# Second attention of a two-layer kernel: VectorE's order of work in a slot, its idle copies, and who makes which keep-mask

## The chip, the cores and the metric

The kernel runs on one core of one Trainium2 chip. The metric is the device time of one execution in microseconds. The engines have queues of their own and run in their order: TensorE (PE in the profile) multiplies matrices, VectorE (DVE), ScalarE (ACT) and GpSimd (POOL) work on elements, and SyncE (SP) starts transfers. They meet only in semaphores, on which an instruction waits and which another one counts up.

## The reference, cut to what matters

The whole model is two layers of attention and a mixture of experts on an input of 4 x 1024 x 128. The change lies in the attention of the second layer, which keeps for each query the best 30% of its keys:

```python
def _L1_attn_ref(x, W_qkv, b_qkv, W_out, b_out):
    ...
    topk = max(1, int(Tx * 0.3))
    ...
    scores = jnp.einsum('bhid,bhjd->bhij', q, k) * scale
    topk_scores, indices = jax.lax.top_k(scores, topk)
    ...
    masked = jnp.full_like(scores, -jnp.inf)
    masked = masked.at[bi, hi, ti, indices].set(topk_scores)
    attn = jax.nn.softmax(masked, axis=-1)
    out = jnp.einsum('bhij,bhjd->bhid', attn, v)
    ...
    return out @ W_out.T + b_out
```

There are 4 sequences of 1024 tokens and 16 heads of 8 columns. A query keeps 307 of 1024 keys.

## The kernel before, in words

Each part of the model is a block in which every engine has its own list of instructions. The second attention is `attention1`. It works on 512 tiles; a tile is one head's 128 queries against all 1024 keys. Every engine runs the same loop over slots, written out at build time: in slot h it does the first step of tile h and later steps of earlier tiles. The constants name the lags: VectorE writes z of tile h-1 (`C2`), finds the tops of tile h-2 (`TOPL`), sorts those of tile h-3 (`SORT`), picks the edge for four tiles up to h-5 (`HIT`) in slots with h % 4 == 0; masks are made for tile h-15 (`PICK`), and TensorE and ScalarE use them for tile h-16 (`TURN`). The order of a slot is written by hand.

A tile goes this way. TensorE makes the scores S (L1134, two buffers). ScalarE counts the scores above a first threshold (L1198); GpSimd makes a better threshold from the count (L1259, L1261). VectorE writes z, the scores minus that threshold, from PSUM to SBUF (L1420). ScalarE counts again, on z (L1205). GpSimd subtracts z from a side value, so that the values nearest to the wanted rank come out on top: these are the near values (L1285, two buffers). VectorE finds the eight largest of each quarter of near (`top`, L1381, four MAX8 instructions) and sorts them: the first eight (`sort_first`, L1395), a match-and-replace that takes them out (`sort_rest`, L1403), the next eight (`sort_last`, L1411). The sort of a tile comes one slot behind its tops. From the sorted list and the count VectorE takes the edge (`hits` L1427, `picked` L1433, `edge` L1439), and GpSimd makes the cut from it (L1266).

The keep-mask of a tile has a large negative value where z is below the cut. VectorE makes it with one tensor_scalar (L1458), ScalarE with one Relu with a steep slope (L1213), with the opposite sign; TensorE adds the mask to the transposed scores by a product with an identity (`k.ident_b`) or with minus an identity (`minus_b`) (L1181, L1182). Before, tiles with an even number have their mask from VectorE, in odd slots, and tiles with an odd number from ScalarE, in even slots. There are four mask buffers. ScalarE then takes the exponential (L1220), and TensorE multiplies with v (L1150); every fourth tile ScalarE copies the sum (L1226), TensorE turns it (L1169) and VectorE normalizes it (`reciprocal` L1484, `ctx` L1491).

Four more pieces stand in these queues. `split_max` on GpSimd (L1242 to L1252, in slots with h % 4 == 0, in front of near) splits the row maxima into three bf16 parts; VectorE transposes them (`flip`, L1468) and SP stores them by four transfers into rows of qs, where TensorE reads them in L1181. Once in eight slots, in those with h % 8 == 6, TensorE sums a check of eight tiles (the flag product, L1162; it waits for VectorE's ctx of the same slot), VectorE reads the sum into a register (`value_load`) and branches on it; the branch was taken once in the profiled execution. `idle` is a small tile that nothing reads; `past_waits` copies one element into it (L1414).

In a slot ScalarE's order is: count of tile h, count of z of tile h-1, mask (if it has one), exponential of tile h-16. TensorE's is: S of tile h, a piece of the products with v, the flag product, the turn of the sums, the masked transposed scores of tile h-16. In the rest of this document "slot 6" is any slot with h % 8 == 6, and so on, and tile 7 any tile with number 7 mod 8.

Of the kernel before, what the change touches and what calls it, by code (L numbers as in the profile page):

```python
# [983 lines left out]
def attention1(nc, k, search, ctx_all):  # L984
# [11 lines left out]
    with ExitStack() as ctx:  # L996
# [70 lines left out]
        tile = lambda hl: base(hl) + hl % PAIR // 4 * P  # L1067
        groups = lambda it, h: it * GU + (h - CHECK - 7) // 8
        closes = lambda it, h: lagged(it, h, CHECK, UN, TOTAL) is not None and (h - CHECK) % 8 == 7

# [50 lines left out]
        def _(pe):  # L1121
# [4 lines left out]
            def slot(it, h):  # L1126
# [43 lines left out]
                if lagged(it, h, TURN, UN, TOTAL) is not None:  # L1170
                    l, hl = nth(it, h, TURN), here(h, TURN)
                    pe.wait_ge(mask_a if hl % 2 else mask_s, it * (UN // 2) + (h - TURN) // 2 + 1)
                    if not (isinstance(l, int) and l == 0):
                        pe.wait_ge(e_done, l)
                    if hl % 4 == 0:
                        pe.wait_ge(top_in, 16 * 4 * (it * QU + (h - TURN) // 4 + 1))
                    if isinstance(l, int) and l == 0:
                        pe.wait_ge(ones_in, 16)
                    for kb in range(IB):
                        block_of = slice(kb * P, (kb + 1) * P)  # L1180
                        pe.matmul(ST[:, block_of], ks[:, base(hl) + kb * P:base(hl) + (kb + 1) * P], qs[:, tile(hl):tile(hl) + P], start=True, stop=False)  # L1181
                        mm = pe.matmul(ST[:, block_of], mask[:, hl % MASKS, block_of],  # L1182
                                       minus_b[:, :] if hl % 2 else k.ident_b[:, :], start=False, stop=True)
                    mm.then_inc(turned, 1)
# [3 lines left out]
        def _(act):  # L1188
            act.wait_ge(pool_const, 4)

            def slot(it, h):
# [8 lines left out]
                if lagged(it, h, C2, UN, TOTAL) is not None:  # L1200
                    l, hl = nth(it, h, C2), here(h, C2) % H
                    act.wait_ge(z_s, l + 1)
                    if not (isinstance(it, int) and l == 0):
                        act.wait_ge(cnt2, l)
                    act.activation(signs[:, 1, :], z[:, hl, :], ACT.Sign, bias=tiny[:, :],  # L1205
                                   accum_out=sgn[1][:, hl:hl + 1]).then_inc(cnt2, 1)
                if lagged(it, h, PICK, UN, TOTAL) is not None and (h - PICK) % 2:
                    l, hl = nth(it, h, PICK), here(h, PICK)
                    act.wait_ge(cut_s, it * QU + (h - PICK) // 4 + 1)
                    act.wait_ge(checked, it * GU + (h - PICK) // 8 + 1)  # L1210
                    if not (isinstance(it, int) and l < MASKS):
                        act.wait_ge(turned, l - (MASKS - 1))
                    act.activation(mask[:, hl % MASKS, :], z[:, hl % H, :], ACT.Relu, bias=cut_steep[:, hl % H:hl % H + 1],  # L1213
                                   scale=-STEEP).then_inc(mask_a, 1)
# [77 lines left out]
        def _(dve):  # L1292
# [74 lines left out]
            def slot(it, h):  # L1367
# [44 lines left out]

                def past_waits(c):
                    dve.tensor_copy(idle[:, 2 * (h % H) + c:2 * (h % H) + c + 1], half[0:1, :])  # L1414

                if has1 is not None:
                    dve.wait_ge(thr1_s, l1 + 1)
                    if h1 % 2 and not (isinstance(it, int) and l1 < H):
                        dve.wait_ge(mask_a, it * (UN // 2) + (h - C2) // 2 - (H // 2 - 1))
                    dve.tensor_scalar(z[:, h1 % H, :], S[h1 % 2][:, :], thr1[:, h1 % H:h1 % H + 1], None, ALU.add, ALU.max,  # L1420
                                      accum_out=zmax[:, h1 % H:h1 % H + 1]).then_inc(z_s, 1)
                if h % 4 == 0:
                    listed()
                    if has4 is not None:
# [3 lines left out]
                                          wide(rank[:, four], WINDOW), ALU.is_equal).then_inc(choice_s, 1)  # L1428
                    sort_first()
                    first_sorted()  # L1430
                    if has4 is not None:
                        dve.wait_ge(choice_s, 2 * q4 + 1)
                        dve.tensor_tensor(picked[:, :, :], hits[:, :, :], best[:, ring4, :], ALU.mult).then_inc(choice_s, 1)  # L1433
                    sort_rest()
                    rest_made()
                    near_made()
                    if has4 is not None:
                        dve.wait_ge(choice_s, 2 * q4 + 2)
                        dve.tensor_reduce(edge[:, four], picked[:, :, :], AX, ALU.add).then_inc(edge_s, 1)  # L1439
                    sort_last()  # L1440
                    top(0)
                    top(1)
# [8 lines left out]
                elif h % 2:  # L1451
                    listed()
                    near_made()
                    if lagged(it, h, PICK, UN, TOTAL) is not None:
                        dve.wait_ge(cut_s, it * QU + (h - PICK) // 4 + 1)
                        if not (isinstance(it, int) and lp < MASKS):
                            dve.wait_ge(turned, lp - (MASKS - 1))
                        dve.tensor_scalar(mask[:, hp % MASKS, :], z[:, hp % H, :], cut[:, hp % H:hp % H + 1], AWAY,  # L1458
                                          ALU.is_lt, ALU.mult).then_inc(mask_s, 1)
                    sort_first()  # L1460
                    top(0)
                    first_sorted()
                    if lagged(it, h, TOPL, UN, TOTAL) is not None and ends(h, TOPL):
                        q, ring = quad(it, h, TOPL), ((h - TOPL) // 4) % 2
                        dve.wait_ge(part_s, PART_STEPS * q + PART_STEPS)
                        if not (isinstance(it, int) and q < 2):
                            dve.wait_ge(top_in, 16 * 4 * (q - 1))
                        dve.transpose(flip[:, ring, :], parts[:, ring, :]).then_inc(flip_s, 1)  # L1468
                    else:
                        past_waits(0)  # L1470
                    sort_rest()
                    top(1)
                    rest_made()
                    past_waits(1)
                    sort_last()
                    top(2)
                    top(3)
                else:
                    q, hn = quad(it, h, NL), here(h, NL + 3) % H
                    norm = lagged(it, h, NL, UN, TOTAL) is not None  # L1480
                    listed()
                    if norm:
                        dve.wait_ge(ot, q + 2)
                        dve.reciprocal(rden[:, hn:hn + 4], heads[:, :, HD]).then_inc(rd, 1)  # L1484
                    sort_first()
                    first_sorted()
                    near_made()
                    if norm:
                        dve.wait_ge(rd, q + 1)
                        dst = ctx_all.rearrange("p t (g c) -> p (t g) c", c=32)[:, bass.ds(q, 1), :].rearrange("p o (j d) -> p (o j) d", d=HD)  # L1490
                        dve.tensor_tensor(dst, heads[:, :, 0:HD], wide(rden[:, hn:hn + 4], HD), ALU.mult).then_inc(normed, 1)  # L1491
                    sort_rest()
                    top(0)
                    rest_made()
                    past_waits(0)
                    sort_last()
                    top(1)
# [6 lines left out]
                    if closes(it, h):  # L1504

                        dve.wait_ge(flag_v, group + 1)
                        past_waits(1)
                        total = dve.value_load(flag_sum[0:1, 0:1].bitcast(I32), min_val=0, max_val=2 ** 31 - 1)
# [742 lines left out]
```

## Time and profile before

| what | value |
|---|---|
| median of three runs | 3609.91 us (3607.0 to 3611.21) |
| profiled execution | 3602.09 us, span 3600.4 us |
| mean granted TensorE clock over the span | 0.779 |
| second attention, first to last z | 1048.3 to 3143.8 us |
| busy over the span: PE, DVE, ACT, POOL | 77%, 76%, 69%, 54% |

The span runs from the first to the last instruction of the profiled execution; its own time is 1.7 us more. A row of the timeline gives the start, the duration, the engine, the line of the kernel, the operation, output<-input with shape and type, and in brackets the idle time of the engine in front of it with what ended it. An instruction's duration can reach beyond the start of the next one on its engine, so a distance from start to start says more of its cost than the duration does. The clock is a share of full speed: 1 is 2.4 GHz, 0.5 is 1.2 GHz.

### The profile page before, as it was taken

Reading aid. Unit: us, or ns where it says so; the run is one execution under the profiler, and the core shown is the slowest. Engines: PE = TensorE matmul, PEld = TensorE weight load, DVE = VectorE, ACT = ScalarE, POOL = GpSimd, SP = SyncE. Lnnn points to the kernel's source line nnn. Section 1 sums busy time; section 2 is a strip of 40 time slices with the busy share of each in tenths; the row PEclk is TensorE's granted clock in tenths of the full one; section 3 lists DMA queues with packets and bytes.
Section 4 is the critical chain, followed back from the end, with each engine's and each line's share of the span. In section 5 each row is a group of like instructions: output and inputs, shape, how many; then the busy total and the mean of one; then the engine's idle time right before and its main releaser. Section 6 shows DMA issues by size and latency. Waiting matters only on the chain. (4 is left out here: it accounts for less than half of the span.)

```text
span 3600.4 us, 75874 instructions
## 1 busy us (share of the span) xinstructions
PE 2754.6 (77%) x23657; PEld 1541.3 (43%) x23705; DVE 2734.2 (76%) x9130; ACT 2480.5 (69%) x4051; POOL 1960.2 (54%) x4543
## 2 busy tenths in 40 slices
PE   4699999677736777777777777776777787757999
PEld 2233333233513454544444545444445454544444
DVE  5777777226448999999999999998999999844444
ACT  2266666433138999999999999997999999832222
POOL 3133333410237777787877777776777777730000
PEclk8699999888656767677777676776776667677999
DMA  5221111010130101101100100110100110010000
GB/s 156 74 53 48 48 53 28 11 33 26 62 54 2 15 3 17 17 2 17 17 7 12 17 14 5 17 15 3 17 11 7 17 15 3 2 31 0 9 6 9
DMA packets 115274, 85.95 MB, mean 24 GB/s; under 512 B 58153, under 2 KB 97339, under 8 KB 114875
## 3 DMA queue, kind: packets, MB, share of 16 engines
q1 hardware_dynamic: 106331, 75.20, 9.7%
q0 software_dynamic: 8192, 4.79, 0.9%
q8 instruction: 185, 3.03, 0.4%
q14 instruction: 214, 1.75, 0.2%
q10 hardware_dynamic: 352, 1.18, 0.1%
HBM read 54.25 MB, written 19.40 MB: 20 GB/s over the span
## 5 line engine op out<-in xcount | busy, mean ns | idle before, releaser
L1285 POOL TENSOR_TENSOR a_near<-a_side,a_z 128x1024 int32<-128x1024 int32 x512 | 968.3, 1891 | 42.7
L1181 PE MATMUL a_ST<-a_qs,a_ks 75*128 75x128 bf16 x4096 | 749.8, 271 | 305.2 <-ACT a_eT L1220 215.3
L1381 DVE MAX8 a_cand<-a_near 128x8 f32<-128x256 f32 x2048 | 778.1, 406 | 2.6 <-POOL a_near L1285 2.5
L1181 PEld LDWEIGHTS a_ST<-a_qs,a_ks 75*128 75x128 bf16 x4096 | 504.8, 125 | 513.7 <-issue 507.0
L1420 DVE TENSOR_SCALAR_CACHE_REDUCE a_z<-a_S,a_thr 128x1024 f32<-128x1024 f32 x512 | 645.6, 1261 | 77.7 <-issue 56.2
L1205 ACT ACTIVATE a_signs<-a_z,a_tiny 128x1024 bf16<-128x1024 f32 x512 | 587.4, 1147 | 152.0 <-DVE a_z L1420 151.2
L1198 ACT ACTIVATE a_signs<-a_S,search 128x1024 bf16<-128x1024 f32 x512 | 569.2, 1112 | 23.1 <-PE a_S L1134 23.0
L1220 ACT ACTIVATE a_eT<-a_ST 128x1024 f32<-128x1024 f32 x512 | 518.7, 1013 | 59.7 <-PE a_ST L1182 59.1
L1134 PE MATMUL a_S<-a_ks,a_qs 72*128 72x512 bf16 x1024 | 438.1, 521 | 99.4 <-DVE a_z L1420 75.6
L775 ACT ACTIVATE a_eT<-a_ST 128x512 f32<-128x512 f32 (+3 forms) x768 | 354.0, 489 | 212.1 <-PE a_ST L745 159.0
L879 DVE TENSOR_REDUCE a_mx<-a_S 128x1 f32<-128x512 f32 (+3 forms) x768 | 380.9, 548 | 92.9 <-PE a_S L732 56.2
L1150 PE MATMUL a_O<-a_eT,a_v 128*9 128x128 f32 x8192 | 404.3, 344 | 1.4 <-ACT wq L1226 1.4
L1182 PE MATMUL a_ST<-ident_b,a_mask 128*128 128x128 bf16 x2048 | 386.1, 277 | 0.0
L1182 PE MATMUL a_ST<-a_minus_b,a_mask 128*128 128x128 bf16 x2048 | 375.4, 271 | 0.0
L1150 PEld LDWEIGHTS a_O<-a_eT,a_v 128*9 128x9 f32 x8192 | 220.4, 107 | 273.0 <-issue 234.6
L1213 ACT ACTIVATE a_mask<-a_z,a_cut_steep 128x1024 bf16<-128x1024 f32 x256 | 290.8, 1136 | 0.0
L1458 DVE TENSOR_SCALAR a_mask<-a_z,a_cut 128x1024 bf16<-128x1024 f32 x256 | 192.5, 752 | 120.0 <-issue 116.4
L1182 PEld LDWEIGHTS a_ST<-ident_b,a_mask 128*128 128x128 bf16 x2048 | 258.9, 126 | 0.1
L1182 PEld LDWEIGHTS a_ST<-a_minus_b,a_mask 128*128 128x128 bf16 x2048 | 253.3, 124 | 0.0
L742 PE MATMUL a_ST<-a_qs,a_ks 128*128 128x512 bf16 (+3 forms) x720 | 232.5, 330 | 18.0 <-ACT a_eT L775 15.0
L2015 ACT ACTIVATE f_gate<-f_G 128x512 f32<-128x512 f32 x112 | 66.8, 597 | 243.5 <-PE f_W L1981 196.0
L1279 POOL TENSOR_TENSOR a_shifted<-a_sgn,a_miss 128x1 f32<-128x1 f32 x512 | 96.3, 188 | 215.1 <-ACT a_signs L1205 214.8
(342 smaller groups left out, 4568.5 us busy)
## 6 DMA issues: line engine op xcount, KB each, us to landing
a_qs<-q_parts SPq DMA_DIRECT2D x174, 64.0 KB
a_ks<-k_parts SPq DMA_DIRECT2D x174, 64.0 KB
a_qs<-a_flip SPq DMA_DIRECT2D x512, 0.8 KB
q_parts<-p_qp SPq DMA_DIRECT2D x48, 128.0 KB, 1.7
k_parts<-p_kp SPq DMA_DIRECT2D x48, 128.0 KB, 1.8
a_qs<-q_parts SPq DMA_DIRECT2D x60, 96.0 KB
a_ks<-k_parts SPq DMA_DIRECT2D x60, 96.0 KB
f_w<-L_ffn_W SPq DMA_DIRECT2D x16, 256.0 KB, 2.9
```

The source lines that it names most:

```text
L775: act.activation(eT[:, gi % 4, p % G, 0:hi - lo], ST[p % 2][:, 0:hi - lo], ACT.Exp, scale=SCALE0).then_inc(e_done, 1)
L879: dve.tensor_reduce(mx[:, lo // CW, col(j) // P + i:col(j) // P + i + 1], S[j][:, 0:hi - lo], AX, ALU.max).then_inc(max_s, 1)
L1134: mm = pe.matmul(S[h % 2][:, lo:lo + CW], qs[0:STACK, tile(h):tile(h) + P], ks[0:STACK, base(h) + lo:base(h) + lo + CW], start=True, stop= ...
L1150: mm = pe.matmul(O[32 * j:32 * j + HD + 1, :], v[:, h0 // PAIR % 2, kb, j * (HD + 1):(j + 1) * (HD + 1)], eT[:, h0 % RING + j, kb * P:(kb ...
L1181: pe.matmul(ST[:, block_of], ks[:, base(hl) + kb * P:base(hl) + (kb + 1) * P], qs[:, tile(hl):tile(hl) + P], start=True, stop=False)
L1182: mm = pe.matmul(ST[:, block_of], mask[:, hl % MASKS, block_of], minus_b[:, :] if hl % 2 else k.ident_b[:, :], start=False, stop=True)
L1198: act.activation(signs[:, 0, :], S[h % 2][:, :], ACT.Sign, bias=first[:, bass.ds(n, 1)], accum_out=sgn[0][:, one]).then_inc(cnt1, 1)
L1205: act.activation(signs[:, 1, :], z[:, hl, :], ACT.Sign, bias=tiny[:, :], accum_out=sgn[1][:, hl:hl + 1]).then_inc(cnt2, 1)
L1220: act.activation(eT[:, hl % RING, :], ST[:, :], ACT.Exp, scale=SCALE1).then_inc(e_done, 1)
L1285: pool.tensor_tensor(near[:, hl % 2, :].bitcast(I32), side[:, one].bitcast(I32).broadcast_to([P, SEQ]), z[:, hl % H, :].bitcast(I32), ALU. ...
L1381: mm = dve.max(found[:, 8 * g:8 * g + 8], near[:, h2 % 2, g * SW:(g + 1) * SW])
L1420: dve.tensor_scalar(z[:, h1 % H, :], S[h1 % 2][:, :], thr1[:, h1 % H:h1 % H + 1], None, ALU.add, ALU.max, accum_out=zmax[:, h1 % H:h1 % H ...
```

## The change

On VectorE, each slot now does the wait for the listed tops and the first sort right behind z. The rest of the front sort (the wait for the first sort and the match-and-replace) follows, and the wait for the near values (`near_made`) comes behind it in all slots; the transpose `flip` of slots with h % 4 == 1 stands in front of it, hits behind it. All copies into `idle` go, but the one in front of the `value_load` of slot 6. ScalarE makes the masks of tiles 1, 3 and 5 of every eight (in slots 0, 2 and 4), VectorE those of the other five (in all odd slots and in slot 6). The waits of TensorE and of VectorE's z on the two mask semaphores count accordingly, and TensorE takes the identity by who made the mask.

```diff
+        by_act = lambda l: l % 2 == 1 and l % 8 != 7
+        acted = lambda l: sum(by_act(x) for x in range(l + 1))
...
-                    pe.wait_ge(mask_a if hl % 2 else mask_s, it * (UN // 2) + (h - TURN) // 2 + 1)
+                    pe.wait_ge(*((mask_a, acted(l)) if by_act(l) else (mask_s, l + 1 - acted(l))))
...
-                                       minus_b[:, :] if hl % 2 else k.ident_b[:, :], start=False, stop=True)
+                                       minus_b[:, :] if by_act(l) else k.ident_b[:, :], start=False, stop=True)
...
-                if lagged(it, h, PICK, UN, TOTAL) is not None and (h - PICK) % 2:
+                if lagged(it, h, PICK, UN, TOTAL) is not None and by_act(nth(it, h, PICK)):
...
-                def past_waits(c):
-                    dve.tensor_copy(idle[:, 2 * (h % H) + c:2 * (h % H) + c + 1], half[0:1, :])
+                def away_made():
+                    if lagged(it, h, PICK, UN, TOTAL) is not None and not by_act(lp):
+                        dve.wait_ge(cut_s, it * QU + (h - PICK) // 4 + 1)
+                        if lp >= MASKS:
+                            dve.wait_ge(turned, lp - (MASKS - 1))
+                        dve.tensor_scalar(mask[:, hp % MASKS, :], z[:, hp % H, :], cut[:, hp % H:hp % H + 1], AWAY,
+                                          ALU.is_lt, ALU.mult).then_inc(mask_s, 1)
...
-                    if h1 % 2 and not (isinstance(it, int) and l1 < H):
-                        dve.wait_ge(mask_a, it * (UN // 2) + (h - C2) // 2 - (H // 2 - 1))
+                    if l1 >= H and by_act(l1 - H):
+                        dve.wait_ge(mask_a, acted(l1 - H))
                     dve.tensor_scalar(z[:, h1 % H, :], S[h1 % 2][:, :], thr1[:, h1 % H:h1 % H + 1], None, ALU.add, ALU.max,
                                       accum_out=zmax[:, h1 % H:h1 % H + 1]).then_inc(z_s, 1)
+                listed()
+                sort_first()
                 if h % 4 == 0:
-                    listed()
+                    first_sorted()
+                    sort_rest()
+                    near_made()
                     if has4 is not None:
...
                         dve.tensor_tensor(hits[:, :, :], odd2[:, :].rearrange("p (o r) -> p o r", o=1).broadcast_to([P, 4, WINDOW]),
                                           wide(rank[:, four], WINDOW), ALU.is_equal).then_inc(choice_s, 1)
-                    sort_first()
-                    first_sorted()
+                    rest_made()
+                    sort_last()
                     if has4 is not None:
...
                         dve.tensor_tensor(picked[:, :, :], hits[:, :, :], best[:, ring4, :], ALU.mult).then_inc(choice_s, 1)
-                    sort_rest()
-                    rest_made()
-                    near_made()
+                    top(0)
                     if has4 is not None:
...
                         dve.tensor_reduce(edge[:, four], picked[:, :, :], AX, ALU.add).then_inc(edge_s, 1)
-                    sort_last()
-                    top(0)
                     top(1)
...
                 elif h % 2:
-                    listed()
-                    near_made()
-                    if lagged(it, h, PICK, UN, TOTAL) is not None:
...
-                    sort_first()
-                    top(0)
-                    first_sorted()
                     if lagged(it, h, TOPL, UN, TOTAL) is not None and ends(h, TOPL):
...
                         dve.transpose(flip[:, ring, :], parts[:, ring, :]).then_inc(flip_s, 1)
-                    else:
-                        past_waits(0)
+                    first_sorted()
                     sort_rest()
-                    top(1)
+                    near_made()
+                    away_made()
                     rest_made()
-                    past_waits(1)
                     sort_last()
-                    top(2)
-                    top(3)
+                    for g in range(SEGS):
+                        top(g)
                 else:
...
-                    listed()
                     if norm:
                         dve.wait_ge(ot, q + 2)
                         dve.reciprocal(rden[:, hn:hn + 4], heads[:, :, HD]).then_inc(rd, 1)
-                    sort_first()
                     first_sorted()
+                    sort_rest()
                     near_made()
                     if norm:
...
                         dve.tensor_tensor(dst, heads[:, :, 0:HD], wide(rden[:, hn:hn + 4], HD), ALU.mult).then_inc(normed, 1)
-                    sort_rest()
+                    away_made()
+                    rest_made()
+                    sort_last()
                     top(0)
-                    rest_made()
-                    past_waits(0)
-                    sort_last()
                     top(1)
                     top(2)
...
-                        past_waits(1)
+                        dve.tensor_copy(idle[:, 2 * (h % H) + 1:2 * (h % H) + 2], half[0:1, :])
```

## Rows read from the trace of the kernel before

**Rows 1.** Stretches: us, busy us (instructions) of each engine, granted clock, DMA share, GB/s

```profile
2000.00:2500.00 500.00, 382.49 (x4214) 246.78 (x4207) 454.54 (x1702) 459.36 (x704) 392.48 (x984) 0.71 0.09 13
...
1648.20:1658.00 9.80, 6.86 (x72) 4.50 (x72) 8.79 (x35) 8.34 (x15) 7.35 (x15) 0.83 0.11 16
2006.20:2016.00 9.80, 8.03 (x69) 4.86 (x61) 8.83 (x33) 7.58 (x13) 6.37 (x13) 0.50 0.05 13
```

**Rows 2.** Waits from 1100 to 3000: us in total, times, longest us

```profile
DVE a_mask L1458 <- issue: 106.9, 173, 1.1
```

**Rows 3.** VectorE's timeline from slot 6 to the next slot 6, lower clock

```profile
2006.21 1.25 DVE L1420 TENSOR_SCALAR_CACHE_REDUCE a_z<-a_S,a_thr 128x1024 f32<-128x1024 f32 x1
...
2007.69 0.19 DVE L1491 TENSOR_TENSOR ctx<-a_OT,a_rden 128x32 f32<-128x32 f32 x1
...
2010.73 1.28 DVE L1420 TENSOR_SCALAR_CACHE_REDUCE a_z<-a_S,a_thr 128x1024 f32<-128x1024 f32 x1 [0.92 <-issue]
...
2015.58 0.80 DVE L1427 TENSOR_TENSOR a_hits<-a_odd,a_rank 128x64 f32<-128x64 f32 x1
...
2020.85 0.75 DVE L1458 TENSOR_SCALAR a_mask<-a_z,a_cut 128x1024 bf16<-128x1024 f32 x1 [0.86 <-issue]
2021.51 0.19 DVE L1395 MAX8 a_best<-a_cand 128x8 f32<-128x32 f32 x1
...
2021.94 0.19 DVE L1468 STREAM_TRANSPOSE a_flip<-a_parts 128x32 bf16<-128x32 bf16 x1
...
2022.19 0.42 DVE L1381 MAX8 a_cand<-a_near 128x8 f32<-128x256 f32 x1
...
2022.58 0.17 DVE L1411 MAX8 a_best<-a_rest 128x8 f32<-128x32 f32 x1
2022.68 0.72 DVE L1381 MAX8 a_cand<-a_near 128x8 f32<-128x256 f32 x2
2023.33 1.25 DVE L1420 TENSOR_SCALAR_CACHE_REDUCE a_z<-a_S,a_thr 128x1024 f32<-128x1024 f32 x1
...
2036.73 0.75 DVE L1458 TENSOR_SCALAR a_mask<-a_z,a_cut 128x1024 bf16<-128x1024 f32 x1 [0.58 <-issue]
...
2039.21 1.25 DVE L1420 TENSOR_SCALAR_CACHE_REDUCE a_z<-a_S,a_thr 128x1024 f32<-128x1024 f32 x1
```

**Rows 4.** GpSimd's timeline in the same period: near and the thr step

```profile
2005.46 1.89 POOL L1285 TENSOR_TENSOR a_near<-a_side,a_z 128x1024 int32<-128x1024 int32 x1
...
2014.40 1.89 POOL L1285 TENSOR_TENSOR a_near<-a_side,a_z 128x1024 int32<-128x1024 int32 x1
...
2018.86 1.89 POOL L1285 TENSOR_TENSOR a_near<-a_side,a_z 128x1024 int32<-128x1024 int32 x1
...
2021.12 0.53 POOL L1261 TENSOR_TENSOR a_thr<-a_scaled,search 128x1 f32<-128x1 f32 x1
```

**Rows 5.** TensorE's timeline in the same period: the flag product

```profile
2008.03 0.75 PE L1162 MATMUL a_OT<-a_signals,ones 128*1 128x176 f32 x2 [1.46 <-DVE ctx L1491]
```

**Rows 6.** ScalarE's timeline in the same period: exp of slot 6, count of slot 2

```profile
2010.64 1.02 ACT L1220 ACTIVATE a_eT<-a_ST 128x1024 f32<-128x1024 f32 x1 [0.85 <-PE a_ST L1182]
...
2024.63 1.15 ACT L1205 ACTIVATE a_signs<-a_z,a_tiny 128x1024 bf16<-128x1024 f32 x1 [0.75 <-DVE a_z L1420]
```

**Rows 7.** VectorE's z in a period at the higher clock

```profile
1648.18 1.25 DVE L1420 TENSOR_SCALAR_CACHE_REDUCE a_z<-a_S,a_thr 128x1024 f32<-128x1024 f32 x1
...
1652.71 1.28 DVE L1420 TENSOR_SCALAR_CACHE_REDUCE a_z<-a_S,a_thr 128x1024 f32<-128x1024 f32 x1 [0.93 <-issue]
...
1680.33 1.25 DVE L1420 TENSOR_SCALAR_CACHE_REDUCE a_z<-a_S,a_thr 128x1024 f32<-128x1024 f32 x1
```

**Rows 8.** ScalarE's timeline in that period: count of tile 6

```profile
1654.04 1.15 ACT L1205 ACTIVATE a_signs<-a_z,a_tiny 128x1024 bf16<-128x1024 f32 x1 [0.28 <-DVE a_z L1420]
```

**Rows 9.** Groups by line on VectorE, 1100 to 3000: xcount, busy us, mean ns, idle

```profile
L1414 DVE COPY a_idle<-a_half 1x1 f32<-1x1 f32 x519 | 63.7, 123 | 0.0
```

**Rows 10.** Groups by line on ScalarE, 1100 to 3000

```profile
L1213 ACT ACTIVATE a_mask<-a_z,a_cut_steep 128x1024 bf16<-128x1024 f32 x231 | 262.3, 1136 | 0.0
```

More of the change, by code:

```diff
@@ L1451, in slot @@
                 elif h % 2:
-                    listed()
-                    near_made()
-                    if lagged(it, h, PICK, UN, TOTAL) is not None:
[L1455 to L1459, printed above, removed]
-                    sort_first()
-                    top(0)
-                    first_sorted()
                     if lagged(it, h, TOPL, UN, TOTAL) is not None and ends(h, TOPL):
@@ L1465, in slot @@
                         dve.wait_ge(part_s, PART_STEPS * q + PART_STEPS)
-                        if not (isinstance(it, int) and q < 2):
+                        if not (isinstance(q, int) and q < 2):
                             dve.wait_ge(top_in, 16 * 4 * (q - 1))
                         dve.transpose(flip[:, ring, :], parts[:, ring, :]).then_inc(flip_s, 1)
-                    else:
-                        past_waits(0)
+                    first_sorted()
                     sort_rest()
-                    top(1)
+                    near_made()
+                    away_made()
                     rest_made()
-                    past_waits(1)
                     sort_last()
-                    top(2)
-                    top(3)
+                    for g in range(SEGS):
+                        top(g)
                 else:
```

## The prediction

> **What bounds the kernel now.** I began with the table of stretches, to see whether one engine fills the second attention. None does: in 500 us VectorE is busy for 454.54, ScalarE for 459.36, GpSimd for 392.48 and TensorE for 382.49, at a granted clock of 0.71 [rows 1]. So work taken from an engine is worth something only where it lies on the chain that paces the loop. The view of waits says what VectorE stands still for: 106.9 us in front of its masks, 173 times in the 1900 us from 1100 to 3000, put down to "issue", that is, to nothing that the view shows [rows 2].
>
> The timelines of one period of eight slots, from z of slot 6 (h mod 8 = 6) to z of the next, name it. They start at 2006.21 and 2039.21, so a period takes 33.00 us [rows 3]. In slot 1 VectorE stands still for 0.86 us and starts its mask at 2020.85; GpSimd makes the near values of tile 7 from 2018.86 for 1.89 us, to 2020.75 [rows 3, 4]. The mask starts 0.10 behind them: the wait called "issue" is the wait for near. Slot 5 has one of 0.58 [rows 3], and 173 waits in some 58 periods are three a period: slots 1, 3 and 5 wait, slot 7 does not.
>
> Followed backwards, the chain of a period is this. VectorE's mask and tops of slot 5 end in z of slot 6; later in that slot comes ctx (2007.69); TensorE's flag product, which stands in front of the transposed scores in its queue, waits 1.46 for ctx and starts at 2008.03 [rows 3, 5]. ScalarE's exp then waits 0.85 for TensorE and starts at 2010.64 [rows 6]. Two counts, the next exp, split_max and near of tile 7 follow, to 2020.75; then mask and tops of slot 1, and z of slot 2 (2023.33), for which ScalarE has waited 0.75 when it counts that tile at 2024.63 [rows 3, 6]. From there ScalarE and GpSimd run on to near of tile 3, and VectorE's mask of slot 5 starts at 2036.73 [rows 3]. Every other queue has slack somewhere in the period; this chain has none.
>
> That holds at the clock's lower level (0.50 in 2006.2 to 2016.0). In the period that starts at 1648.18 the clock is 0.83 [rows 1], and ScalarE waits not for TensorE but for z of slot 7: that z starts at 1652.71, 4.53 behind slot 6's, and the count of tile 6 at 1654.04, after waiting 0.28 [rows 7, 8]. The next period starts at 1680.33: it took 32.15 [rows 7]. So what VectorE does in slot 6 is on the chain as a whole at the higher clock, and at the lower only up to ctx. A mean clock of 0.71 between the levels 0.5 and 1 means 58% of the time at the lower; the mean period is 0.58 x 33.00 + 0.42 x 32.15 = 32.64.
>
> **The change, part by part.** All prices are distances from start to start.
>
> *Sort in front, idle copies out, slots 1 and 5.* Today 2.48 us lie between the start of the mask and the next z (2020.85 to 2023.33; 2036.73 to 2039.21 [rows 3]). Afterwards mask (0.66, 2020.85 to 2021.51), last sort (0.10, 2022.58 to 2022.68) and four tops (two take 0.65, 2022.68 to 2023.33, so 1.30) are left: 2.06. What moves ahead, the first sort (0.10 like the last), transpose and match (0.25, 2021.94 to 2022.19 [rows 3]), takes 0.35, less than the wait that hides it. The gain on the chain is 0.42 in each of the two slots, 0.84 a period. Slot 3 gains as much, but slot 4 then waits for near of tile 2, which ScalarE's queue makes no earlier: counted at nothing; without that wait it would be another 0.42. The moved transpose releases SP's four stores of the row maxima about 0.4 earlier; TensorE needs them fourteen slots later, so nothing waits for them.
>
> *Idle copies.* The 519 copies last 123 ns each [rows 9], but cost less: a top and a copy take 0.39 (2022.19 to 2022.58 [rows 3]) and a top alone half of 0.65, so a copy takes 0.06; nearly nine a period are 0.5. Those of slots 1 and 5 are in the 0.42; the others stand in slots with slack: nothing. Without one, an instruction that needs the sort just issued can start as late as that sort's end, 0.19 behind its start [rows 3], instead of 0.10. The near wait hides that in slots 1, 3 and 5; uncovered it costs 0.09 a slot.
>
> *Slot 6.* near of tile 4 ends 1.14 behind z today (2005.46 + 1.89 = 2007.35 [rows 4]), and ctx starts at 1.48. As VectorE's slot 5 becomes 0.42 shorter and near comes no earlier against it, near will end at about 1.52 and ctx start at 1.61, 0.13 later. From ctx to z of slot 7 today takes 3.04 (2007.69 to 2010.73 [rows 3]); the match leaves (about half of 0.25), a copy leaves (0.06), a mask comes in (0.66): 3.51, so z of slot 7 starts 5.12 behind slot 6's, where today's two periods have 4.52 and 4.53: 0.59 later.
>
> *The mask taken from ScalarE.* One of four a period, 1136 ns [rows 10]. It lies in slot 6, in front of the exp that waits 0.85 for TensorE at the lower clock [rows 6], or of the count that waits for z of slot 7 at the higher [rows 8]. ScalarE only waits longer, so I take nothing; if neither wait were there it would be up to 1.14.
>
> *New waits.* In slots 0 and 4 the near wait moves in front of hits. Today hits takes 0.80 from 2015.58, to 2016.38, 0.09 behind the end of near (2014.40 + 1.89 = 2016.29 [rows 3, 4]): it is held by GpSimd already, so this is a hold that becomes a wait. Behind it stand picked, edge and the tops, whose reader, GpSimd's cut, comes a slot later.
>
> *Mask against GpSimd.* The thr step beside slot 1's mask took 0.53 from 2021.12 [rows 4], while that mask ran to 2021.60. The Trainium skill ("SBUF — State Buffer", section "SBUF: two separate sides") says that VectorE's instructions in a two-port mode or with two SBUF inputs share an exclusive lock with GpSimd's, and the loser blocks for the whole instruction; the traced hits and thr agree. By that rule the 64 added masks each hold GpSimd. What such a hold can cost here lies between nothing and the 0.53 of that step a period. I take nothing: it falls in slot 6, in front of near of tile 5, which slot 7 needs, where no mask waits today although z comes 0.59 earlier than it will.
>
> *Sum.* Lower clock: +0.13 - 0.84 = -0.71. Higher clock: +0.59 - 0.84 = -0.25. Mean 0.58 x 0.71 + 0.42 x 0.25 = 0.52 a period. Of 64 periods the first two have no masks: 62 x 0.52 = 32 us. The profiled execution took 3602.1 (span 3600.4), so it would take 3570; the median of the runs shown is 7.8 above it, 3609.9, so I forecast **3578**. If every period came to the lower level it would be 32.29 against 32.64, -22 us (3588); all at the higher, 31.90, -46 us (3564). That is the likeliest case's own range.
>
> **Rivals.**
> - *Held transpose (no change).* In the new order the transpose runs while near is being made. If it were held as hits is, transpose and match (0.25) would come behind near again: 0.17 gained a slot instead of 0.42. Lower clock -0.21, higher +0.25, mean -0.02, -1 us: 3609. For it: hits. Against it: nothing in these rows.
> - *Held sort (slower).* If the whole front sort were held until near ends, 2.06 + 0.25 + 0.10 = 2.41 would stay behind it, 0.07 gained a slot: lower clock -0.01, higher +0.45, mean +0.18, +11 us: 3621. At the higher clock it decides once less than 0.30 of the 0.42 is saved. Against it: hits has two SBUF inputs, the sort's instructions one.
> - *VectorE alone sets the pace.* Were ScalarE's relief to bring near forward everywhere, the near waits (106.9 in 58 periods, 1.84) and copies (0.5) would go and a mask (0.66) come: -1.68 a period, -104 us: 3506. Against it: the chain runs through split_max and near, which lose nothing.
> - *GpSimd held by the added mask, on the chain (no change).* +0.53 x 62 = 33 us on the forecast: 3611.
>
> **Chances.** Forecast 0.55, held transpose 0.13, held sort 0.16, VectorE alone 0.10, GpSimd held 0.06. Under 0.2% (7 us) a measurement of this kernel can't tell from no change. Faster 0.55 + 0.10 = 0.65, same 0.13 + 0.06 = 0.19, slower 0.16. The range, 3550 to 3622, leaves out VectorE alone and the far ends of the rest.
>
> **What the profile would show.** Right: slots 1 and 5 take 2.06 from mask to z; the waits in front of the masks of slots 1, 3 and 5 shrink by about 0.4 but stay, and one appears in slot 4; z of slot 7 comes about 5.1 behind slot 6's; ScalarE waits about 1 us longer in slot 6, though it makes fewer masks; a period takes 32.3 or 31.9. Wrong: a transpose or match longer than 0.2 us while near runs; near waits gone; near of tile 5 late for slot 7; a granted clock well away from 0.71.

## The result, and the profile after

The changed kernel takes 3582.59 us (median of 4 runs, 3578.21 to 3583.92) against 3608.45 for the kernel before (4 runs beside it, 3606.57 to 3611.21): a ratio of 0.9926, with a 95% interval of 0.9908 to 0.9943. It is faster by 26 us; the forecast was 32. The profiled execution took 3578.21 (span 3576.5).

Nearly all of it lies where the prediction put it: from z of slot 6 in the second period to z of slot 6 in the last, 62 periods, the second attention took 2041.41 us before and takes 2016.75 now, 24.66 less; the two spans differ by 23.9. Without the first period and the one with the taken branch, a period takes 32.20 in the mean instead of 32.60.

The table of stretches of the changed kernel (stretch, length, then busy time and count of instructions of PE, PEld, DVE, ACT and POOL, the granted clock, the DMA share and GB/s), in the columns of [rows 1]:

```profile
1500.00:2000.00 500.00, 374.93 (x4278) 241.61 (x4278) 459.73 (x1617) 450.44 (x698) 410.64 (x995) 0.73 0.08 11
...
1995.40:2005.20 9.80, 6.75 (x56) 4.36 (x57) 8.87 (x29) 6.52 (x12) 7.28 (x13) 0.65 0.02 6
2028.00:2037.80 9.80, 6.38 (x70) 4.28 (x70) 8.67 (x29) 7.26 (x12) 7.14 (x13) 0.83 0.11 18
```

VectorE is a little busier (459.73 in 500 us against the 454.54 of [rows 1], with less idle filler and one mask more a period), ScalarE less (450.44 against 459.36). The clock is about where it was: 0.73 here, and before 0.71 in [rows 1] and 0.75 from 1500 to 2000. The two lower rows are the first 9.8 us of two neighbouring periods, one that begins at a lower clock and one at a higher.

The view of waits of the changed kernel, 1100 to 3000 (who waits, for whom, us, times, the longest), answers to [rows 2]:

```profile
DVE a_mask L1420 <- POOL a_near L1287: 49.5, 117, 1.0
...
DVE a_hits L1438 <- POOL a_near L1287: 24.1, 58, 0.4
DVE ctx L1485 <- POOL a_near L1287: 20.5, 114, 0.3
```

The wait that was called "issue" now carries its name, near. It went from 106.9 us and 173 times to 49.5 and 117, two a period instead of three; a new one of 0.4 a period stands in front of hits, in slot 4.

VectorE's timeline of the period that answers to [rows 3], and of the next one:

```profile
1995.44 1.26 DVE L1427 TENSOR_SCALAR_CACHE_REDUCE a_z<-a_S,a_thr 128x1024 f32<-128x1024 f32 x1
...
1997.38 0.19 DVE L1485 TENSOR_TENSOR ctx<-a_OT,a_rden 128x32 f32<-128x32 f32 x1 [0.27 <-POOL a_near L1287]
1997.49 0.75 DVE L1420 TENSOR_SCALAR a_mask<-a_z,a_cut 128x1024 bf16<-128x1024 f32 x1
...
2009.38 0.19 DVE L1464 STREAM_TRANSPOSE a_flip<-a_parts 128x32 bf16<-128x32 bf16 x1
2009.50 0.09 DVE L1405 MATCH_VALUE_LOAD a_rest<-a_best,a_cand 128x8 f32 x1
2009.58 0.17 DVE L1405 MATCH_REPLACE8 a_rest<-a_best,a_cand 128x32 f32<-128x32 f32 x1
2010.47 0.75 DVE L1420 TENSOR_SCALAR a_mask<-a_z,a_cut 128x1024 bf16<-128x1024 f32 x1 [0.71 <-POOL a_near L1287]
...
2012.54 1.27 DVE L1427 TENSOR_SCALAR_CACHE_REDUCE a_z<-a_S,a_thr 128x1024 f32<-128x1024 f32 x1
...
2017.55 0.75 DVE L1420 TENSOR_SCALAR a_mask<-a_z,a_cut 128x1024 bf16<-128x1024 f32 x1
...
2021.71 0.23 DVE L1438 TENSOR_TENSOR a_hits<-a_odd,a_rank 128x64 f32<-128x64 f32 x1 [0.42 <-POOL a_near L1287]
...
2025.91 0.75 DVE L1420 TENSOR_SCALAR a_mask<-a_z,a_cut 128x1024 bf16<-128x1024 f32 x1 [0.46 <-POOL a_near L1287]
...
2027.98 1.27 DVE L1427 TENSOR_SCALAR_CACHE_REDUCE a_z<-a_S,a_thr 128x1024 f32<-128x1024 f32 x1
...
2029.83 0.19 DVE L1485 TENSOR_TENSOR ctx<-a_OT,a_rden 128x32 f32<-128x32 f32 x1 [0.18 <-POOL a_near L1287]
...
2033.31 1.28 DVE L1427 TENSOR_SCALAR_CACHE_REDUCE a_z<-a_S,a_thr 128x1024 f32<-128x1024 f32 x1 [0.92 <-issue]
...
2060.03 1.26 DVE L1427 TENSOR_SCALAR_CACHE_REDUCE a_z<-a_S,a_thr 128x1024 f32<-128x1024 f32 x1
```

GpSimd's near of tile 7 in slot 1, and its thr step beside the added mask of slot 6:

```profile
2008.54 1.89 POOL L1287 TENSOR_TENSOR a_near<-a_side,a_z 128x1024 int32<-128x1024 int32 x1
...
2030.17 0.56 POOL L1263 TENSOR_TENSOR a_thr<-a_scaled,search 128x1 f32<-128x1 f32 x1
```

The first period takes 32.54 (1995.44 to 2027.98), the second 32.05. In slots 1 and 5 mask to z takes 2.07 (2010.47 to 2012.54, 2025.91 to 2027.98), against 2.48. The transpose and the match run beside near of tile 7, which GpSimd makes from 2008.54 to 2010.43, at 0.19 and 0.17: nothing holds them. Slot 3's mask (2017.55) has no wait any more. In slot 6, ctx comes 1.94 behind z in the first period and 1.85 in the second, against 1.48. The 1.85 is the rule: of the 60 periods of the trace that have a ctx there, 59 have it at 1.84 or 1.85, and the period shown first is the one exception. Lower-clock periods of the usual kind take 32.45. In the second period z of slot 7 comes 5.33 behind slot 6's (2027.98 to 2033.31), against 4.53.

ScalarE's exp in slot 6 and its count of tile 6 in the two periods, which answer to [rows 6, 8]:

```profile
2000.32 1.02 ACT L1222 ACTIVATE a_eT<-a_ST 128x1024 f32<-128x1024 f32 x1 [2.33 <-PE a_ST L1184]
...
2034.64 1.15 ACT L1207 ACTIVATE a_signs<-a_z,a_tiny 128x1024 bf16<-128x1024 f32 x1 [0.47 <-DVE a_z L1427]
```

The mask that ScalarE lost became a wait for TensorE of 2.33 instead of 0.85 in the first kind of period. In the second, the count still starts 1.33 behind z of slot 7, as before: it goes with VectorE.

### The profile page after: what moved, and what is told of

The parts are those of the page before. It is cut to its first block and busy times, and to the rows that moved or that the text cites. A ratio compares the mean times of both kernels' runs of the same rounds, so it can differ in the third digit from the quotient of the medians.

```text
span 3576.5 us, 74689 instructions
## 1 busy us (share of the span) xinstructions
PE 2730.8 (76%) x23705; PEld 1518.9 (42%) x23705; DVE 2730.8 (76%) x8652; ACT 2416.1 (68%) x3987; POOL 2005.5 (56%) x4543
## 5 line engine op out<-in xcount | busy, mean ns | idle before, releaser
L1183 PE MATMUL a_ST<-a_qs,a_ks 75*128 75x128 bf16 x4096 | 723.3, 265 | 319.1 <-ACT a_eT L1222 185.7
L1383 DVE MAX8 a_cand<-a_near 128x8 f32<-128x256 f32 x2048 | 740.4, 411 | 2.6 <-POOL a_near L1287 2.6
L1184 PE MATMUL a_ST<-ident_b,a_mask 128*128 128x128 bf16 x2560 | 475.0, 274 | 0.0
L1184 PEld LDWEIGHTS a_ST<-ident_b,a_mask 128*128 128x128 bf16 x2560 | 320.2, 125 | 0.0
L1420 DVE TENSOR_SCALAR a_mask<-a_z,a_cut 128x1024 bf16<-128x1024 f32 x320 | 239.8, 750 | 57.8 <-POOL a_near L1287 53.7
L742 PE MATMUL a_ST<-a_qs,a_ks 128*128 128x512 bf16 (+3 forms) x768 | 247.2, 334 | 15.7 <-ACT a_eT L775 12.9
L1184 PE MATMUL a_ST<-a_minus_b,a_mask 128*128 128x128 bf16 x1536 | 258.8, 257 | 0.0
L1261 POOL TENSOR_TENSOR a_scaled<-a_sgn,search 128x1 f32<-128x1 f32 x512 | 171.6, 335 | 144.9 <-ACT a_signs L1200 143.4
L1215 ACT ACTIVATE a_mask<-a_z,a_cut_steep 128x1024 bf16<-128x1024 f32 x192 | 219.5, 1143 | 0.0
L1184 PEld LDWEIGHTS a_ST<-a_minus_b,a_mask 128*128 128x128 bf16 x1536 | 178.8, 116 | 0.1
```

The costliest lines, as they stand in the source:

```text
L1383: mm = dve.max(found[:, 8 * g:8 * g + 8], near[:, h2 % 2, g * SW:(g + 1) * SW])
```

## The experiments

Each kernel's ratio is to the kernel before on the same chip (3609.79, 3606.99 and 3609.33 us for the three groups of runs: the first four, the next four, the last).

**The order without the new share.** The changed kernel, with masks alternating as before.

```diff
-        by_act = lambda l: l % 2 == 1 and l % 8 != 7
+        by_act = lambda l: l % 2 == 1
```

> The changed kernel with the masks shared as before: ScalarE makes those of tiles 1, 3, 5 and 7 again, VectorE none in slot 6. Chain theory: ScalarE's relief in slot 6 was worth nothing and VectorE's mask there costs at the higher clock, where slot 6 lies on the chain as a whole. z of slot 7 comes 0.66 us earlier (about 4.7 behind slot 6's instead of 5.35). A period stays 32.45 at the lower clock and falls from 32.05 to about 31.4 at the higher: -0.3 on the mean over 62 periods, about 3564 us against 3583 of the changed kernel. Balance theory (the relief of ScalarE is what made the kernel faster, the order little): slower than the changed kernel, 3600 or more.

3563.91 us, ratio 0.9871 (0.9856 to 0.9886), as expected. VectorE's z in a higher-clock period of it (the clock is 0.83 from 1865.9 to 1868.9):

```profile
1864.40 1.27 DVE L1427 TENSOR_SCALAR_CACHE_REDUCE a_z<-a_S,a_thr 128x1024 f32<-128x1024 f32 x1
...
1869.09 1.29 DVE L1427 TENSOR_SCALAR_CACHE_REDUCE a_z<-a_S,a_thr 128x1024 f32<-128x1024 f32 x1 [0.95 <-issue]
...
1895.80 1.26 DVE L1427 TENSOR_SCALAR_CACHE_REDUCE a_z<-a_S,a_thr 128x1024 f32<-128x1024 f32 x1
```

z of slot 7 is back at 4.69 behind slot 6's, and the period takes 31.40; at the lower clock it takes 32.45, as with the new share.

**The share without the order.** The kernel before, with `by_act`, `acted` and the waits of the diff, and slot 6's mask behind ctx.

> The kernel before, order and idle copies as they were, with only the masks shared anew: ScalarE three of eight, VectorE five, the added one in slot 6 behind ctx. Chain theory: lower clock +0.1 a period, higher +0.66 (z of slot 7 later), mean +0.33 x 62 = +20 us, about 3629 us, slower than before by 0.5%. Balance theory: faster than before, by 10 us or more.

3627.66 us, ratio 1.0048 (1.0034 to 1.0062): slower, as expected. Together the two runs say that the order is worth some 46 us and that the share costs 18 to 20 of them.

**ctx in front of the near wait in slots 2 and 6.**

```diff
-                    near_made()
                     if norm:
...
+                    near_made()
                     away_made()
```

> The changed kernel with the wait for the near values moved behind ctx in the slots that normalize (2 and 6); nothing else differs. Chain theory: ctx of slot 6 starts 1.6 us behind z instead of 1.94, the flag product and the exponential behind it come 0.35 earlier, so a period at the lower clock falls from 32.45 to 32.1; at the higher clock only the 0.1 of ctx itself is saved: mean -0.24 x 62 = -15 us, about 3568 us. Rival (the flag product is not on the chain, the low-clock period is set elsewhere): within 4 us of the changed kernel's 3583.

3567.62 us, ratio 0.9886 (0.987 to 0.9901), as expected. VectorE's z and ctx of a lower-clock period, then ScalarE's exp in it:

```profile
1798.60 1.27 DVE L1427 TENSOR_SCALAR_CACHE_REDUCE a_z<-a_S,a_thr 128x1024 f32<-128x1024 f32 x1
...
1800.19 0.18 DVE L1484 TENSOR_TENSOR ctx<-a_OT,a_rden 128x32 f32<-128x32 f32 x1
...
1830.80 1.27 DVE L1427 TENSOR_SCALAR_CACHE_REDUCE a_z<-a_S,a_thr 128x1024 f32<-128x1024 f32 x1
```

```profile
1803.11 1.02 ACT L1222 ACTIVATE a_eT<-a_ST 128x1024 f32<-128x1024 f32 x1 [1.96 <-PE a_ST L1184]
```

ctx starts 1.59 behind z instead of 1.85, and exp still 2.92 behind ctx (2.94 in the changed kernel, 2.95 before); the period falls from 32.45 to 32.20. At the lower clock the place of ctx sets the period, as the prediction's chain has it.

**VectorE's added mask in slot 2 instead of slot 6** (tile 3's instead of tile 7's).

```diff
-        by_act = lambda l: l % 2 == 1 and l % 8 != 7
+        by_act = lambda l: l % 2 == 1 and l % 8 != 3
```

> The changed kernel with another mask moved: VectorE makes that of tile 3 (in slot 2) instead of tile 7 (in slot 6), ScalarE those of tiles 1, 5 and 7. The share is still three and five. Chain theory: slot 6 loses 0.66 (higher clock -0.63 a period, lower nothing); in slot 2 ScalarE's mask stood on the chain between the count of tile 1 and that of tile 2, so up to 1.04 goes there, but z of slot 3 comes 0.66 later and takes most of it: -0.1 at either clock. Mean -0.4 x 62 = -25 us, about 3558 us. Balance theory: no difference to the changed kernel, 3583, since the work of each engine is the same.

3578.25 us, ratio 0.9914 (0.9899 to 0.9929): a miss, 20 us above the expected. Each kind of period is as short as expected, 32.34 and 31.0 to 31.3, but 46 of 61 were of the longer kind and 12 of the shorter. Its table of stretches shows the clock beside it, 0.68 and 0.70 where the changed kernel has 0.73:

```profile
1100.00:1500.00 400.00, 315.79 (x3367) 197.95 (x3367) 367.08 (x1292) 363.07 (x558) 325.86 (x796) 0.68 0.08 10
1500.00:2000.00 500.00, 392.10 (x4279) 245.11 (x4279) 460.06 (x1623) 454.69 (x700) 408.87 (x995) 0.70 0.08 11
```

**ctx first, with masks alternating** (the third edit and the first).

> The two edits that helped, together: the changed kernel's order and no idle copies, the near wait behind ctx in slots 2 and 6, and the masks shared as before (ScalarE four of eight). Chain theory: the two gains lie at different clock levels and add: lower clock 32.45 - 0.35 = 32.1, higher 31.4 or a little under. With half of the periods at either level 31.75 against 32.60 before, 62 x -0.85 = -53 us, about 3556 us. Rival (behind ctx another link is just as late, so that the gains don't add): 3564, like the order alone.

3539.75 us, ratio 0.9815 (0.9802 to 0.9828), 16 below the expected. The longer periods take 32.17, near the expected 32.1; the shorter ones take 31.1 to 31.3, up to 0.3 less than the 31.4 that was expected as the upper end. Of 61 periods 27 are of the shorter kind and 15 of the longer; the others lie between.

**ctx first, with the added mask in slot 2** (the third edit and the fourth).

> The changed kernel with the near wait behind ctx and VectorE's extra mask that of tile 3 (slot 2) instead of tile 7. With tile 3 alone the periods were 31.26 at the higher clock and 32.34 at the lower, but five of six came to the lower level, and that was all its gain. Chain theory: 32.34 - 0.36 = 31.98 at the lower level, 31.2 at the higher; if the shares of the levels stay, 31.85 a period, 62 x -0.75 = -46 us, about 3563 us; if half of the periods come to the higher level, 3547 us. Rival (the place of the mask sets the time, ctx nothing): 3578.

3528.79 us (3524.0 to 3533.2), ratio 0.9784 (0.977 to 0.9797): the fastest version here, 2.2% under the kernel before, and 18 us below the lower of the two times expected. Periods take 31.96 (27 of 61) or 30.87 to 31.1 (29), the latter up to 0.3 less than the expected 31.2. Its clock over a long stretch is no higher than that of the fourth experiment:

```profile
1100.00:2480.00 1380.00, 1100.04 (x11854) 686.96 (x11855) 1285.00 (x4526) 1265.08 (x1944) 1163.28 (x2767) 0.68 0.08 12
```

So the mean clock alone does not tell how many periods are short. The clock in slot 6 does, while TensorE works between ctx and exp. These are the 3 us from 1.5 to 4.5 us behind z of slot 6, in a period of 30.87 and in one of 31.96 of this kernel (columns as above):

```profile
1629.80:1632.80 3.00, 2.48 (x36) 1.50 (x36) 2.27 (x11) 3.00 (x5) 2.60 (x7) 1.00 0.32 49
1692.00:1695.00 3.00, 2.57 (x19) 1.95 (x20) 2.28 (x12) 2.10 (x3) 2.60 (x7) 0.50 0.00 0
```

In that stretch the clock is 1.00 in all 29 of the short periods and 0.50 in all 27 of the long ones; in the fourth run it is 1.00 in the 12 short ones and 0.50 to 0.59 in the 46 long ones.

**The new order in slots 1 and 5 alone.** The kernel before, with first sort, transpose and match in front of the near wait there, and without the copy there; the copies of the other slots and the alternating masks stay.

```diff
+                elif h % 4 == 1:
+                    listed()
+                    sort_first()
...
+                    first_sorted()
+                    sort_rest()
+                    near_made()
...
+                    rest_made()
+                    sort_last()
+                    for g in range(SEGS):
+                        top(g)
                 elif h % 2:
```

> The kernel before with the new order in slots 1 and 5 alone (first sort, transpose, match, near wait, mask, last sort, four tops; the copy there goes); slots 0, 2, 3, 4, 6 and 7 keep their order and their idle copies, and the masks are shared as before. Chain theory: only these two slots are on the chain behind a near wait, so this gives all that the whole new order gives without the new share: 0.8 a period less ctx's later start, about 3564 us. Rival (the gain comes from all slots, a part from each): 3587, half of the way.

3568.58 us, ratio 0.9898 (0.9883 to 0.9914). Expected was all that the whole new order gives. By ratio it is 1.0% of 1.3%, and the two intervals just overlap: most of it, and all of it is not excluded.

**No idle copies, all else as before** (the one ahead of the register load stays).

```diff
-                    else:
-                        past_waits(0)
...
-                    past_waits(1)
...
-                    past_waits(0)
```

> The kernel before with the idle copies taken out but for the one in front of the register load; order and shares as they were. Chain theory: one copy of 0.06 in each of slots 1 and 5 lies on the chain, at the higher clock also the one in slot 6: -0.12 to -0.18 a period, -8 to -11 us, unless the sort's next step then starts later by as much; about 3601 us, between 3598 and 3610. Rival (copies hide the waits): slower than before.

3599.68 us (11 runs), ratio 0.9983 (0.9974 to 0.9992): 6 to 7 us, as two copies of 0.06 on the chain in 62 periods make (7.4).

**One idle copy put back behind near in slots 1 and 5.** The changed kernel, and in front of the mask:

```diff
                     near_made()
+                    if h % 4 == 1:
+                        dve.tensor_copy(idle[:, 2 * (h % H):2 * (h % H) + 1], half[0:1, :])
                     away_made()
```

> The changed kernel with one idle copy put between the near wait and the mask in slots 1 and 5. In the changed kernel the mask starts 0.04 us behind near, so GpSimd's next step (scaled) meets it and takes 0.73, and near of tile 4 ends 3.93 behind near of tile 3 instead of 3.72: that made ctx of slot 6 late. If that hold is the cause, the copy (0.06) lets scaled through first: scaled 0.2, thr 0.5, near of tile 4 at 3.72 to 3.75, ctx of slot 6 at 1.75 to 1.8 behind z instead of 1.94, though VectorE does more. The time changes little: two copies cost 0.12 a period, the earlier ctx gives 0.15 to 0.2 back at the lower clock alone: 3583 to 3588 us. If the hold has nothing to do with it: near of tile 4 keeps its 3.93, and the time rises by 0.12 x 62 = 7 us.

3575.06 us, ratio 0.9904 (0.9888 to 0.9921): 8 us under the expected, and not slower than the changed kernel (0.9908 to 0.9943), though an instruction was added to the chain twice a period. In the mean a period takes 32.15 (32.20 in the changed kernel), which is 3 us of the difference; the rest is not told from noise, as the intervals overlap. GpSimd's timeline around slot 5 says why; first the kernel before, then the changed one, then this one, with VectorE's mask and the ctx behind it:

```profile
2034.74 1.89 POOL L1285 TENSOR_TENSOR a_near<-a_side,a_z 128x1024 int32<-128x1024 int32 x1
...
2036.74 0.19 POOL L1259 TENSOR_TENSOR a_scaled<-a_sgn,search 128x1 f32<-128x1 f32 x1
2037.00 0.53 POOL L1261 TENSOR_TENSOR a_thr<-a_scaled,search 128x1 f32<-128x1 f32 x1
...
2038.46 1.89 POOL L1285 TENSOR_TENSOR a_near<-a_side,a_z 128x1024 int32<-128x1024 int32 x1
```

```profile
2023.98 1.89 POOL L1287 TENSOR_TENSOR a_near<-a_side,a_z 128x1024 int32<-128x1024 int32 x1
2025.83 0.19 POOL L1290 TENSOR_TENSOR a_rank<-a_sgn,a_shifted 128x1 f32<-128x1 f32 x1
2025.97 0.73 POOL L1261 TENSOR_TENSOR a_scaled<-a_sgn,search 128x1 f32<-128x1 f32 x1
2026.79 0.19 POOL L1263 TENSOR_TENSOR a_thr<-a_scaled,search 128x1 f32<-128x1 f32 x1
...
2027.91 1.89 POOL L1287 TENSOR_TENSOR a_near<-a_side,a_z 128x1024 int32<-128x1024 int32 x1
```

```profile
2022.83 1.89 POOL L1287 TENSOR_TENSOR a_near<-a_side,a_z 128x1024 int32<-128x1024 int32 x1
...
2024.82 0.19 POOL L1261 TENSOR_TENSOR a_scaled<-a_sgn,search 128x1 f32<-128x1 f32 x1
2025.09 0.55 POOL L1263 TENSOR_TENSOR a_thr<-a_scaled,search 128x1 f32<-128x1 f32 x1
...
2026.58 1.89 POOL L1287 TENSOR_TENSOR a_near<-a_side,a_z 128x1024 int32<-128x1024 int32 x1
```

```profile
2024.84 0.76 DVE L1420 TENSOR_SCALAR a_mask<-a_z,a_cut 128x1024 bf16<-128x1024 f32 x1
...
2026.91 1.27 DVE L1427 TENSOR_SCALAR_CACHE_REDUCE a_z<-a_S,a_thr 128x1024 f32<-128x1024 f32 x1
...
2028.51 0.19 DVE L1487 TENSOR_TENSOR ctx<-a_OT,a_rden 128x32 f32<-128x32 f32 x1
```

In the changed kernel the mask starts at 2025.91, 0.06 ahead of the scaled step, which then takes 0.73, and from near of tile 3 to near of tile 4 it is 3.93. With the copy the mask starts at 2024.84, 0.02 behind the scaled step; that step takes 0.19, the one after it 0.55, and near to near is 3.75 (3.72 before: 2034.74 to 2038.46). ctx starts 1.60 behind z, near the 1.61 of the prediction. Of the 0.25 by which that is earlier, 0.18 is near's; the rest is z, which comes later because the mask now starts 0.12 behind near instead of 0.04.

## Why the prediction was right, and which terms were off

**The chain of near waits: right.** Of the order's gain the two slots 1 and 5 give most on their own (the seventh run), and each shortens from mask to z by 0.41, for which 0.42 was forecast. The copies are worth 0.06 each on the chain (the eighth run), and slot 4, where hits now waits 0.42 and then takes 0.23, costs nothing that any run shows.

**ScalarE's relief and slot 6's added mask: right.** The first two runs part them: the share alone is slower by 18 us and, taken out of the change, gives 20 back (0.0055 by the two ratios). ScalarE's free time became a wait for TensorE. From ctx to z of slot 7 takes 3.48 (2029.83 to 2033.31), for which 3.51 was forecast.

**ctx of slot 6: the term that was mis-sized.** Forecast +0.13 behind z, measured +0.37 in nearly all periods (1.85 against 1.48) and +0.46 in the one shown first. A slip in the sum is a small part of it: near at 1.14 and 0.42 later is 1.56, not 1.52, so +0.17 would have followed from its own rows. The step that failed is "I take nothing" for a hold of GpSimd by a mask. The prediction looked for the hold under the added mask, in slot 6, and bounded it by the 0.53 of the thr step. There it came, 0.56 for the thr step at 2030.17, and cost nothing, as forecast: in no period of the trace does slot 7's mask wait for near. The hold that cost came under a mask that was there before, slot 5's. In the new order VectorE starts that mask 0.04 behind near instead of 0.10. The seventh run has the 0.04 too and the eighth has 0.09, so it comes with the order of slots 1 and 5 and not with the missing copies; why is not shown. The mask then starts 0.06 ahead of GpSimd's scaled step, where it had started 0.01 ahead (2036.73 and 2036.74), and that step is held for 0.73 instead of 0.19: it ends at 2026.70, just behind the mask (2026.66). No semaphore stands between the two instructions, so here two engines meet otherwise than in a semaphore. The thr step behind it, held for 0.53 before (2037.00), is free again at 0.19. The one costs 0.54 and the other gives back 0.34, so near of tile 4 comes 0.21 later (3.93 against 3.72), and ctx behind it; z of slot 7, forecast at 5.12 behind slot 6's, comes at 5.33 for the same reason. The ninth run moves the mask's start back, and scaled step and near come back with it. The Trainium skill ("SBUF — State Buffer", section "SBUF: two separate sides") has a lock that one side takes while the other blocks for the whole instruction; the 0.73 beside a mask of 0.75 agrees.

**How the sum comes out.** In the period shown, against that of [rows 3]: ctx +0.46; exp to the end of near of tile 7 as before (10.11); from there to z of slot 2, 2.11 instead of 2.58; to slot 5's mask 13.37 instead of 13.40; mask to z 2.07 instead of 2.48; with 0.01 less from ctx to exp that is -0.46, and the period fell from 33.00 to 32.54; with ctx at its usual 1.85 it is -0.55, to 32.45. At the higher clock: +0.80 to z of slot 7, -0.47 from near of tile 7 to z of slot 2, and -0.03 and -0.41 as above, so -0.11, and the period fell from 32.15 to 32.05. The forecast had -0.71 and -0.25. In the mean, 0.40 instead of 0.52 a period: 25 us instead of 32. Two things in this are luck. The masks' earlier start behind near, which was not forecast, gives back 0.07 a period (0.47 and 0.44 where twice 0.42 was forecast) of what the late ctx takes. And the share of 58% at the lower clock, read from a mean clock, gave a mean period of 32.64 where the trace has 32.60, though the periods before are not of two lengths only: of 61, 24 take 33.0, 25 take 31.9 to 32.3, and the others mostly lie between.

**Slot 3's wait: wrong, at no cost.** It was to shrink but stay, and it has gone (2017.55 has none). The period did not shorten for it, as the chain does not run there.

**The rivals.** Held transpose and held sort fell at the 0.19 and 0.17 beside near. VectorE alone as the bound fell too: 1.6 us of near waits a period remain (49.5 + 24.1 + 20.5 in some 59 periods). The held GpSimd was partly true, by another mask than the added one and for 0.21 a period where it is on the chain.

**What stays open.** The share of the two kinds of period. The expectations were right to about 0.1 us for the longer kind, and up to 0.3 too long for the shorter one in the fifth and sixth runs. The fourth run missed because most of its periods were of the longer kind; the fifth and the sixth came out faster in part because the shorter kind was shorter than expected, the fifth also because it had more of it. A period is short where the clock in slot 6 is at the higher level (1.00 against 0.50 in the rows of the sixth run), and the mean clock does not give the share (0.68 in a kernel with half of the periods short, 0.68 to 0.70 in one with a fifth); why the sixth run finds the higher level there more often than the fourth was not settled. That the better place of the added mask, slot 2, is worth something only with ctx moved as well rests on the times of the fourth to sixth runs alone.

## What to carry to other kernels

Work taken from an engine counts only where it stands behind the wait that paces the loop: moving three short instructions in front of that wait in two of eight slots, and dropping the copy there, gave at least as much as the whole change did (ratio 0.9898 against 0.9926, with intervals that just overlap). When a piece is moved, look at both sides of it, at what the next engine's small steps now meet a few hundredths earlier and at what stands behind the moved wait (ctx here); a part of a change that pays for nothing can hide inside one that is faster in total, so time the parts apart.

## What had not been expected of the hardware

A start 0.06 us earlier on VectorE, against near, cost more than it saved: the 128x1 step on GpSimd took 0.73 instead of 0.19 when the mask began 0.06 ahead of it, and an added copy of one element made up for itself. And the loop has two main lengths of period, with others between: 32.45 and 32.05 us in the changed kernel, 31.96 and 30.87 in the fastest one. They follow one another within one execution, by the clock that is granted in slot 6, so that a kernel whose every kind of period is shorter (the fourth run's, 32.34 and 31.26, beside the first run's 32.45 and 31.40) can still be the slower, 3578 against 3564 us.
